# Softmax attention on one core: scores in two accumulated layers of 48 rows, two heads in the two halves of the rows

## The chip, the cores and the metric

One core of one Trainium2 chip runs the whole program in one launch. The metric is the device time of that execution in microseconds (us); lower is better. The engines are named as the profile names them: PE is TensorE (PEld its weight loads), DVE is VectorE, ACT is ScalarE, POOL is GpSimd, SP is SyncE, which only issues transfers here.

## The reference, cut to what matters

The program is four blocks on x of shape (16, 512, 256): softmax attention, a mixture of experts, a gated linear attention, and the mixture of experts again. The change is in the first block alone:

```
q, k, v = (proj(Wq), proj(Wk), proj(Wv))      # 16 heads of 16 dimensions
q, k = _apply_rope(q, k, cos, sin)
scores = jnp.einsum('bhqd,bhkd->bhqk', q, k) / jnp.sqrt(jnp.float32(dk))
attn = jax.nn.softmax(scores, axis=-1)
out = jnp.einsum('bhqk,bhkd->bhqd', attn, v)
return out.transpose(0, 2, 1, 3).reshape(B, S, D) @ Wo.T
```

## The kernel before, in words

`attention_project` normalises x, projects it, rotates q and k, and stores each as three bf16 parts (high, middle, low) whose sum is the fp32 value. `attention_mix` does the rest and is where the change lies.

**Operands.** A product of q and k in nearly fp32 precision is the sum of six products of parts. `Q_PARTS` and `K_PARTS` list the six pairs; each takes 16 rows (the head's dimensions) of the tiles `qs` and `ks`, [128 rows, 16 heads, 512 tokens] in bf16. The first three slots are 48 rows and alone give the maxima; all six are 96 rows. `ROW` puts the slots of even heads at rows 0 to 95, and those of odd heads at 64 to 111 (the first three) and 0 to 47 (the others). Two more rows hold the high and low part of the row maximum in `qs` and -1 in `ks`, so that the score comes out with the maximum subtracted; `SHIFT_ROW` says where. Scores are so a single bf16 product over 98 rows (even heads) or 112 rows (odd heads, some of them filled with -1 times 0): `K_ALL`.

**Steps.** The unit is a pair of heads (even, odd) of a sequence; there are 16 times 8 pairs, and a step of the loop works on several pairs at once, each stage with its own lag in steps (`walk_pairs`). Every engine runs its own list of stages in a written order, and semaphores tie them together. In a step PE does, in this order: `max_products(0)`, two scores, `turn_output` (every second step), `mix_values(1)`, `turn_shift` (every fourth step), `max_products(1)`, two scores, `max_products(2)`, two scores, `mix_values(0)`, `max_products(3)`, two scores, and in single steps `turn_att` and `project`.

- `max_products(t)` (L621): two bf16 products of 48 rows by 512 columns, the even head in rows 0 to 47, the odd one in rows 64 to 111, side by side into two PSUM banks. DVE's `maxima(t)` (L718) reduces both with one instruction.
- `scores(i)` (L649): i is 0 to 3 for the even head's four blocks of 128 keys and 4 to 7 for the odd head's. Each fills one PSUM bank of 512 columns; ACT's `exponentials(i)` (L778) takes the exponential of that bank.
- `mix_values` (L664): four fp32 products side by side, each with 32 output rows.
- `turn_output` (L677), `turn_shift` (L633), `turn_att` (L690), `project` (L703): transposes and the projection of the output, fp32.

**PSUM.** All eight banks are in use: two double banks `ps_m` (maxima, transposed output and shift, projection), three banks `ps_s` (scores, transposed attention), one for `mix_values`. `M_ORDER` and `S_ORDER` give the order in which the users of the two rings take their turn. A user of turn n waits until turn n - 2 (`M_RING`) or n - 3 (`S_RING`) has been drained by DVE or ACT. Each score waits so for itself.

**Transfers.** SP loads the parts of the next sequence while the present one runs, into the other of two tile sets (`first_qs`, `first_ks`, and the two halves of `second`), and, together with POOL, moves the maxima (`m_parts`) into their rows. POOL fills the constant rows of the first set with three memsets (L541 to L543) and ACT those of the second set with three copies.

Of the kernel before, what the change touches and what calls it, by code (L numbers as in the profile page):

```python
# [64 lines left out]

# [269 lines left out]
def attention_mix(nc, dram, x_in, x_out, const):  # L335
# [13 lines left out]

    SHIFT_ROW = (96, 48)  # L350
    K_ALL = (98, 112)

# [14 lines left out]
    M_RING, S_RING = 2, 3  # L367
    M_ORDER = [("max0", 0, 1, 0), ("output", L_OTURN, 2, 1), ("shift", L_TURN, 4, 3), ("max1", 0, 1, 0), ("max2", 0, 1, 0), ("max3", 0, 1, 0),
               ("out0", L_OUT[0], PAIRS, PAIRS - 1), ("out1", L_OUT[1], PAIRS, PAIRS - 1)]
    S_ORDER = [(f"score{i}", L_S, 1, 0) for i in range(8)] + [(f"att{q}", L_ATT[q], PAIRS, PAIRS - 1) for q in range(2)]  # L370
    M_AT, S_AT = turns_in_order(M_ORDER, TOTAL + 16), turns_in_order(S_ORDER, TOTAL + 16)
    M_PERIOD, S_PERIOD = 2 * (4 * PAIRS + 2 + PAIRS // 2 + 2), 2 * (8 * PAIRS + 2)

    with ExitStack() as ctx:
        def sb(name, shape, dt=fp32):
            return ctx.enter_context(nc.sbuf_tensor("a2_" + name, shape, dt))
# [7 lines left out]
        woT = sb("woT", [P, 2, D])  # L384
        fill = sb("fill", [P, 2])
        ident, wo_rows = const["ident_sb"], const["wo_rows"]
        qs = [const["first_qs"], const["second"][:, 0:H * S].rearrange("p (h t) -> p h t", h=H)]
        ks = [const["first_ks"], const["second"][:, H * S:].rearrange("p (h t) -> p h t", h=H)]
        vs = sb("vs", [P, QT, D])
# [84 lines left out]
        def _(sp):  # L474
# [7 lines left out]
            def load_m(seq, u, f):  # L482
                wait(sp, m_drained, m_turn("shift", seq.ahead(4 * f + 3 + L_TURN)) + 1)
                for r in range(2):
                    row, at = SHIFT_ROW[0] + r, r * 4
                    sp.dma_start(qs[u][row:row + 1, f * HALF:(f + 1) * HALF:2, :], m_parts[at:at + 4, f, :]).then_inc(m_even_loaded[f], 16)

            def sequence(seq, b, u, last):
# [5 lines left out]
                if not last:  # L494
                    scores_read(before, 0)
                    load_qk(b + 1, 1 - u, 0, range(MAX_SLOTS), first_loaded)
                    if first:
                        sp.wait_ge(rows_set[1], 3)
                    load_qk(b + 1, 1 - u, 0, range(MAX_SLOTS, len(Q_PARTS)), rest_loaded)
# [14 lines left out]

            sp.wait_ge(rows_set[0], 3)
            for f in range(2):
# [17 lines left out]
        def _(pool):  # L534
            def heads_of(u):
                return va[u][:].rearrange("p t (h w) -> p t h w", w=VW)

            for k, value in enumerate((-1.0, 0.0)):
                nc.gpsimd.memset(fill[:, k:k + 1], value).then_inc(fill_set, 1)
            pool.wait_ge(fill_set, 2)  # L540
# [24 lines left out]
            def load_odd(n, step):  # L565
                if n.k % 4 != 3:
                    return
                f = n.p // 4
                pool.wait_ge(m_drained, m_turn("shift", step) + 1)
                if f == 0 and isinstance(n.base, int):  # L570
                    pool.wait_ge(rows_set[n.u], 3)
                passed_by(pool, pool_passed)
                for r in range(2):
                    row, at = SHIFT_ROW[1] + r, HALF + r * 4
                    pool.dma_start(qs[n.u][row:row + 1, f * HALF + 1:(f + 1) * HALF:2, :], m_parts[at:at + 4, f, :]).then_inc(m_odd_loaded[f], 16)

# [29 lines left out]
        def _(pe):  # L606
# [5 lines left out]
            def max_products(t):  # L612
                def stage(n, step):
                    u = n.u
                    if n.p % 4 == 0 and t == 0:
                        wait(pe, first_loaded[u][n.p // 4], 16 * 4 * MAX_SLOTS * (n.base + u))
                    name = f"max{t}"
                    wait(pe, m_drained, m_turn(name, step) + 1 - M_RING)
                    for e in range(2):
                        rows = slice(ROW[e][0], ROW[e][0] + MAX_SLOTS * DK)  # L620
                        last = nc.tensor.matmul(m_bank(name, step)[:, e, :], qs[u][rows, 2 * n.p + e, t * P:(t + 1) * P], ks[u][rows, 2 * n.p + e, :],  # L621
                                                start=True, stop=True)
                    last.then_inc(m_filled, 1)
                return stage
# [10 lines left out]

            def scores(i):
                def stage(n, step):
                    u, e, t = n.u, i // QT, i % QT
                    if n.p % 4 == 0 and i == 0:
                        f = n.p // 4  # L640
                        pe.wait_ge(rest_loaded[u][f], 16 * 4 * (len(Q_PARTS) - MAX_SLOTS) * (n.base + n.k // PERIOD + 1))
                        pe.wait_ge(rows_set[u], 3)
# [51 lines left out]
            def project(q):  # L694
                def stage(n, step):
# [5 lines left out]
                    for t in range(2):  # L701
                        for c in range(2):
# [3 lines left out]

            walk_pairs(pe, [(0, max_products(0)), (L_S, scores(0)), (L_S, scores(1)), (L_OTURN, turn_output), (L_MIX + 1, mix_values(1)),
                            (L_TURN, turn_shift), (0, max_products(1)), (L_S, scores(2)), (L_S, scores(3)), (0, max_products(2)), (L_S, scores(4)), (L_S, scores(5)), (L_MIX, mix_values(0)),
                            (0, max_products(3)), (L_S, scores(6)), (L_S, scores(7)),
                            (L_ATT[0], turn_att(0)), (L_ATT[1], turn_att(1)), (L_OUT[0], project(0)), (L_OUT[1], project(1))])  # L710

        @block.vector
        def _(dve):
# [29 lines left out]
            def residual(q):  # L743
                def stage(n, step):
# [3 lines left out]
                    if q == 0:  # L748
# [5 lines left out]

            walk_pairs(dve, [(0, maxima(0)), (L_OTURN, normalise), (L_TURN, copy_shift), (0, maxima(1)), (0, maxima(2)), (0, maxima(3)),
                             (L_OUT[0], residual(0)), (L_OUT[1], residual(1))], unrolled=2)

        @block.scalar
        def _(act):
            act.wait_ge(w_turned, 1)  # L760
            nc.scalar.activation(woT[:], ps_s[0][:].rearrange("p (c a) -> p c a", c=2), ACT.Copy).then_inc(w_copied, 1)

            act.wait_ge(fill_set, 2)
            for k in range(2):
                act.wait_ge(const["parts_stored"][k], 16 * SEQS // 2)
            for to, at, k in ((ks[1], slice(32, 64), 0), (qs[1], slice(32, 64), 1), (ks[1], slice(96, 98), 0)):
                heads = to[at, 1 if at.start == 32 else 0::2, :]
                source = fill[at, k:k + 1].rearrange("p (h t) -> p h t", h=1).to_broadcast([at.stop - at.start, H // 2, S])
                nc.scalar.activation(heads, source, ACT.Copy).then_inc(rows_set[1], 1)
# [27 lines left out]
            walk_pairs(act, [(L_S, exponentials(0)), (L_S, exponentials(1)), (L_OCOPY, copy_output)]  # L797
                       + [(L_S, exponentials(i)) for i in range(2, 8)] + [(L_ATT[0], copy_att(0)), (L_ATT[1], copy_att(1))])

# [1249 lines left out]
def program(nc, a):  # L2049
# [37 lines left out]
    with nc.cleanup_on_exit(), ExitStack() as ctx:  # L2087
# [6 lines left out]
        ahead_x = landing["ahead_x"] = ctx.enter_context(nc.sbuf_tensor("ahead_x", [P, WD], fp32))  # L2094
        with (nc.sbuf_tensor("first_qs", [P, 16, S], bf16) as first_qs, nc.sbuf_tensor("first_ks", [P, 16, S], bf16) as first_ks,
              nc.sbuf_tensor("second", [P, 2 * 16 * S], bf16) as second):
# [58 lines left out]
```

## Time and profile before

| | |
|---|---|
| time, three runs | 2562.98 us median, 2553.72 to 2566.74 |
| the profiled execution, span from first to last instruction | 2572.4 us (its time outside the span isn't listed) |
| mean granted TensorE clock | 0.958 of full speed |
| busy over the span | PE 93%, DVE 63%, ACT 53%, POOL 45% |
| attention_mix | about 235 to 1098 us of the span |

A profile row of the timeline gives the start, the duration (to the end of the last of a merged group), the engine, the line of the kernel, and the count behind an x; in brackets stands the idle time before it and what ended it. Matmuls of one engine are pipelined: the start of the next, not the listed end, says when PE was free again.

### The profile page before, as it was taken

To read this page: it belongs to the slowest core of one execution; us is meant where nothing else is said; L and a number is where in the kernel's file an instruction comes from. 1 tells how busy PE (TensorE), PEld (TensorE's weight loads), DVE (VectorE), ACT (ScalarE), POOL (GpSimd) and SP (SyncE) were. 2 spreads that over 40 slices of the span, in tenths; PEclk is the share of its full clock that TensorE was granted. 3 is DMA by queue.
4 is the path that set the end of the run, shared out by engine and by line. 5 is a ranking of instruction groups with operands and counts; after the bars stand their busy time and mean duration, and the time that the engine had idled before them with its cause. 6 is when DMAs were issued, how large, how long until landed. Compare 5 with 4: busy or idle time off the path is not lost. (4 is left out here: it accounts for less than half of the span.)

```text
span 2572.4 us, 48366 instructions
## 1 busy us (share of the span) xinstructions
PE 2397.5 (93%) x14822; PEld 1294.4 (50%) x14822; DVE 1621.6 (63%) x3733; ACT 1370.4 (53%) x2772; POOL 1154.1 (45%) x1497
## 2 busy tenths in 40 slices
PE   8997999999999999979998996999999969998997
PEld 5663233333333333356556764566666645555765
DVE  6777888888888888455552323677777746543332
ACT  5665677667766776646532322555555436532322
POOL 6997110111111111133226775777777723324776
PEclk9997899999999999988998998999999988898999
DMA  6654423232323231145766884011111026585886
GB/s 187 217 189 161 122 81 105 78 107 78 103 82 103 82 99 61 38 132 186 239 220 189 241 197 77 18 38 38 35 38 34 20 75 204 183 283 155 223 228 109
DMA packets 286870, 325.20 MB, mean 126 GB/s; under 512 B 30496, under 2 KB 272368, under 8 KB 286704
## 3 DMA queue, kind: packets, MB, share of 16 engines
q1 hardware_dynamic: 252928, 274.22, 34.0%
q0 software_dynamic: 29184, 46.43, 8.9%
q10 hardware_dynamic: 4592, 2.47, 0.4%
q8 instruction: 89, 1.46, 0.2%
q14 instruction: 77, 0.63, 0.1%
HBM read 217.29 MB, written 105.19 MB: 125 GB/s over the span
## 5 line engine op out<-in xcount | busy, mean ns | idle before, releaser
L718 DVE TENSOR_REDUCE a_row_max<-a_ps_m 128x2 f32<-128x1024 f32 x512 | 607.4, 1219 | 84.2 <-PE a_ps_m L621 79.3
L778 ACT ACTIVATE a_probs<-a_ps_s 128x512 f32<-128x512 f32 x1024 | 536.8, 601 | 206.5 <-PE a_ps_s L649 206.1
L664 PE MATMUL a_ps_o<-a_probs,a_va 128*32 128x512 f32 x2048 | 272.9, 606 | 0.8 <-ACT a_o_sb L787 0.8
L1750 POOL TENSOR_TENSOR b_spread<-b_decay,held_own_sb 128x512 f32<-128x512 f32 x256 | 267.9, 1079 | 8.6 <-DVE b_weight L1811 8.6
L1811 DVE TENSOR_TENSOR b_weight<-b_ps_s,b_spread 128x512 f32<-128x512 f32 x256 | 163.6, 681 | 9.0 <-PE b_ps_s L1952 9.0
L649 PE MATMUL a_ps_s<-first_qs,first_ks 98*128 98x512 bf16 (+1 forms) x512 | 160.8, 395 | 3.3 <-DMA first_qs<-a_m_parts 3.3
L649 PE MATMUL a_ps_s<-second 98*128 98x512 bf16 (+1 forms) x512 | 156.4, 385 | 4.8 <-DMA second<-a_m_parts 2.4
L558 POOL CAST a_high<-a_row_max 128x32 bf16<-128x32 f32 x32 | 6.6, 206 | 316.0 <-DVE a_row_max L718 316.0
L599 POOL DMA_DIRECT2D x<-a_xo x32 | 24.2, 755 | 273.7 <-DVE a_xo L752 271.3
L317 PE MATMUL a_ps_qk<-a_w_qk,a_xnT 128*128 128x512 f32 x256 | 122.2, 600 | 0.0
L1560 DVE SCALAR_TENSOR_TENSOR m2e_h<-m2e_act_g,m2e_xg,m2e_ps_h 128x192 f32<-128x192 f32 x64 | 26.5, 414 | 144.3 <-ACT m2e_act_g L1489 110.8
L1560 DVE SCALAR_TENSOR_TENSOR m1e_h<-m1e_act_g,m1e_xg,m1e_ps_h 128x192 f32<-128x192 f32 x64 | 26.5, 414 | 141.7 <-ACT m1e_act_g L1489 123.0
L621 PE MATMUL a_ps_m<-first_ks,first_qs 48*128 48x512 bf16 x512 | 106.4, 413 | 10.0 <-DVE a_row_max L718 9.3
L621 PEld LDWEIGHTS a_ps_m<-first_ks,first_qs 48*128 48x128 bf16 x512 | 24.7, 93 | 158.2 <-issue 90.5
L1214 PE MATMUL m1f_ps_h<-m_kept,held_ws_gate_up_sb 128*128 128x512 f32 x192 | 104.2, 679 | 0.0
L1888 ACT ACTIVATE b_o_sb<-b_ps_o,held_b_den_eps 128x512 f32<-128x512 f32 x64 | 44.1, 688 | 111.4 <-PE b_ps_o L1962 111.4
L1214 PE MATMUL m2f_ps_h<-m_kept,held_ws_gate_up_sb 128*128 128x512 f32 x192 | 101.7, 665 | 0.0
L621 PE MATMUL a_ps_m<-second 48*128 48x512 bf16 x512 | 99.8, 386 | 0.4
L621 PEld LDWEIGHTS a_ps_m<-second 48*128 48x128 bf16 x512 | 24.5, 92 | 147.6 <-issue 94.8
L1828 DVE TENSOR_TENSOR b_xo<-b_ps_w,b_xt 128x256 f32<-128x256 f32 x63 | 26.8, 425 | 93.4 <-PE b_ps_w L1987 93.4
L200 POOL TENSOR_TENSOR a_qk<-a_rot_cos,a_rot_sin 128x512 f32<-128x512 f32 x64 | 81.4, 1272 | 7.9 <-DVE a_rot_sin L234 7.9
L649 PEld LDWEIGHTS a_ps_s<-second 98*128 98x128 bf16 (+1 forms) x512 | 37.8, 97 | 83.9 <-issue 38.0
(393 smaller groups left out, 5410.4 us busy)
## 6 DMA issues: line engine op xcount, KB each, us to landing
parts<-second SPq DMA_DIRECT2D x16, 1536.0 KB, 6.2
second<-parts SPq DMA_DIRECT2D x384, 64.0 KB
rows<-m_early SPq DMA_DIRECT2D x32, 640.0 KB
m_early<-x SPq DMA_DIRECT2D x31, 512.0 KB
first_qs<-parts SPq DMA_DIRECT2D x192, 64.0 KB, 3.5
first_ks<-parts SPq DMA_DIRECT2D x192, 64.0 KB, 2.9
m_own<-in_L_ffn_w_gate_dram SPq DMA_DIRECT2D x24, 384.0 KB, 6.6
m_own<-in_L_ffn_w_up_dram SPq DMA_DIRECT2D x24, 384.0 KB, 7.2
```

The source lines that it names most:

```text
L200: nc.gpsimd.tensor_tensor(qk[:, u, :], rot_cos[:, u, :], rot_sin[:, u, :], ALU.add).then_inc(qk_done, 1)
L317: last = nc.tensor.matmul(ps_qk[u][:], xnT[:, u, c, :], w_qk[:, c, :], start=c == 0, stop=c == 1)
L621: last = nc.tensor.matmul(m_bank(name, step)[:, e, :], qs[u][rows, 2 * n.p + e, t * P:(t + 1) * P], ks[u][rows, 2 * n.p + e, :], start=Tru ...
L649: nc.tensor.matmul(s_bank(name, step)[:], ks[u][0:K_ALL[e], h, t * P:(t + 1) * P], qs[u][0:K_ALL[e], h, :], start=True, stop=True).then_in ...
L664: last = nc.tensor.matmul(ps_o[VW * j:VW * (j + 1), :], va[n.u][:, t, (h0 + j) * VW:(h0 + j + 1) * VW], probs[:, group % 2, j, t, :], star ...
L718: nc.vector.tensor_reduce(row_max[:, n.k // 4 % 2, t, :, n.p % 4], m_bank(name, step)[:], AX.X, ALU.max).then_inc(m_drained, 1)
L778: nc.scalar.activation(probs[:, group % 2, j, t, :], s_bank(name, step)[:], ACT.Exp, scale=DK ** -0.5).then_inc(s_drained, 1)
L1214: last = nc.tensor.matmul(ps_h[i][:], w_gu[:, c, i, :], x_turned[:, kept_at(r), c, :], start=c == 0, stop=c == 1)
L1560: nc.vector.scalar_tensor_tensor(h[:, i % 2, j, :], act_g[:, i % 2, j, :], xg[:, i % XB, j, D + e:D + e + 1], ps_h[j][:, 1, :], ALU.mult, ...
L1750: nc.gpsimd.tensor_tensor(spread[:, n % 2, heads].rearrange("p h t c -> p (h t) c"), decay[:, n % 3, heads].rearrange("p h (t o) -> p (h t ...
L1811: nc.vector.tensor_tensor(weight[:, n % 2, heads, :], ps_s[r][:].rearrange("p h (j t) -> p (h j) t", t=P), spread[:, n % 2, heads].rearran ...
L1888: nc.scalar.activation(o_sb[:, n % 2, :], ps_o[:].rearrange("p i a -> p (i a)"), ACT.Identity, bias=den_eps[:]).then_inc(o_copied, 1)
```

## The change

Scores are no longer one product over 98 or 112 rows. The six slots of a head now lie in two layers, three slots each: layer 0 has the slots of the maxima, layer 1 the other three and the two shift rows. Even heads have rows 0 to 47 (to 49 in layer 1), odd heads 64 to 111 (to 113), so that a pair's tile is [group, layer, token]. `scores(t)` does the four products of both heads for one block of keys, layer 0 of both and then layer 1 of both, accumulated in the two heads' banks. The wait for the ring now stands once, ahead of the four, for the turn of the second bank. The order of the score turns becomes even, odd, even, odd. The stages of PE are put in another order (`turn_att`, `project` and `mix_values(0)` come between the third scores and `max_products(3)`), and with it the orders of the rings, of DVE and of ACT. Two memsets and two copies fill the constant rows instead of three and three.

```diff
-ROW = ((0, 16, 32, 48, 64, 80), (64, 80, 96, 0, 16, 32))
+LAYERS = 2
+EDGE = 64
...
-                row = ROW[e][slot]
-                yield tile[row:row + 16, f * 8 + e:(f + 1) * 8:2, :], src[e]
+                row = EDGE * e + slot % MAX_SLOTS * 16
+                yield tile[row:row + 16, f * 4:(f + 1) * 4, slot // MAX_SLOTS, :], src[e]
...
-    SHIFT_ROW = (96, 48)
-    K_ALL = (98, 112)
+    PART_ROWS = MAX_SLOTS * DK
+    FILL_ROW = 32
...
-    M_ORDER = [("max0", 0, 1, 0), ("output", L_OTURN, 2, 1), ("shift", L_TURN, 4, 3), ("max1", 0, 1, 0), ("max2", 0, 1, 0), ("max3", 0, 1, 0),
-               ("out0", L_OUT[0], PAIRS, PAIRS - 1), ("out1", L_OUT[1], PAIRS, PAIRS - 1)]
-    S_ORDER = [(f"score{i}", L_S, 1, 0) for i in range(8)] + [(f"att{q}", L_ATT[q], PAIRS, PAIRS - 1) for q in range(2)]
+    M_ORDER = [("max0", 0, 1, 0), ("output", L_OTURN, 2, 1), ("shift", L_TURN, 4, 3), ("max1", 0, 1, 0), ("max2", 0, 1, 0),
+               ("out0", L_OUT[0], PAIRS, PAIRS - 1), ("out1", L_OUT[1], PAIRS, PAIRS - 1), ("max3", 0, 1, 0)]
+    S_ORDER = ([(f"score{i}", L_S, 1, 0) for i in range(6)] + [(f"att{q}", L_ATT[q], PAIRS, PAIRS - 1) for q in range(2)]
+               + [(f"score{i}", L_S, 1, 0) for i in range(6, 8)])
...
-            nc.gpsimd.memset(ks[0][32:64, 1::2, :], -1.0).then_inc(rows_set[0], 1)
-            nc.gpsimd.memset(qs[0][32:64, 1::2, :], 0.0).then_inc(rows_set[0], 1)
-            nc.gpsimd.memset(ks[0][96:98, 0::2, :], -1.0).then_inc(rows_set[0], 1)
-            pool.wait_ge(rows_set[0], 3)
+            for e in range(2):
+                at = slice(EDGE * e + FILL_ROW, EDGE * (e + 1))
+                nc.gpsimd.memset(ks[0][at, :, 1, :], -1.0).then_inc(rows_set[0], 1)
+            pool.wait_ge(rows_set[0], 2)
...
-                    name = f"score{i}"
-                    wait(pe, s_drained, s_turn(name, step) + 1 - S_RING)
-                    h = 2 * n.p + e
-                    nc.tensor.matmul(s_bank(name, step)[:], ks[u][0:K_ALL[e], h, t * P:(t + 1) * P], qs[u][0:K_ALL[e], h, :],
-                                     start=True, stop=True).then_inc(s_filled, 1)
+                    names = [f"score{2 * t + e}" for e in range(2)]
+                    wait(pe, s_drained, s_turn(names[1], step) + 1 - S_RING)
+                    for layer, shift_rows in ((0, 0), (1, 2)):
+                        for e in range(2):
+                            rows = slice(EDGE * e, EDGE * e + PART_ROWS + shift_rows)
+                            last = nc.tensor.matmul(s_bank(names[e], step)[:], ks[u][rows, n.p, layer, t * P:(t + 1) * P], qs[u][rows, n.p, layer, :],
+                                                    start=layer == 0, stop=layer == 1)
+                            if layer == 1:
+                                last.then_inc(s_filled, 1)
...
-            walk_pairs(pe, [(0, max_products(0)), (L_S, scores(0)), (L_S, scores(1)), (L_OTURN, turn_output), (L_MIX + 1, mix_values(1)),
-                            (L_TURN, turn_shift), (0, max_products(1)), (L_S, scores(2)), (L_S, scores(3)), (0, max_products(2)), (L_S, scores(4)), (L_S, scores(5)), (L_MIX, mix_values(0)),
-                            (0, max_products(3)), (L_S, scores(6)), (L_S, scores(7)),
-                            (L_ATT[0], turn_att(0)), (L_ATT[1], turn_att(1)), (L_OUT[0], project(0)), (L_OUT[1], project(1))])
+            walk_pairs(pe, [(0, max_products(0)), (L_S, scores(0)), (L_OTURN, turn_output), (L_MIX + 1, mix_values(1)), (L_TURN, turn_shift),
+                            (0, max_products(1)), (L_S, scores(1)), (0, max_products(2)), (L_S, scores(2)),
+                            (L_ATT[0], turn_att(0)), (L_ATT[1], turn_att(1)), (L_OUT[0], project(0)), (L_OUT[1], project(1)), (L_MIX, mix_values(0)),
+                            (0, max_products(3)), (L_S, scores(3))])
...
-                    group, j, t = n.k // 2, 2 * (n.k % 2) + i // QT, i % QT
+                    group, j, t = n.k // 2, 2 * (n.k % 2) + i % 2, i // 2
```

DVE's list moves the two `residual` stages ahead of `maxima(3)`, ACT's the two `copy_att` stages ahead of the last two exponentials. The transfers of parts and maxima keep their number and size and go to the new places.

## Rows read from the trace of the kernel before

**Rows 1.** The page: span, and section 1, busy time of each engine.
```profile
span 2572.4 us, 48366 instructions
...
PE 2397.5 (93%) x14822; PEld 1294.4 (50%) x14822; DVE 1621.6 (63%) x3733; ACT 1370.4 (53%) x2772; POOL 1154.1 (45%) x1497
```
**Rows 2.** Windows 320 to 1040 us: all work, then L621 alone; clock, DMA share, GB/s last.
```profile
320.00:1040.00 720.00, 714.18 (x4218) 230.33 (x4214) 593.42 (x612) 504.31 (x970) 88.97 (x224) 1.00 0.30 88
...
320.00:1040.00 720.00, 172.85 (x888) 42.51 (x888) 1.00 0.30 88
```
**Rows 3.** Groups by line, 320 to 1040 us: busy us, mean ns, then idle before.
```profile
L778 ACT ACTIVATE a_probs<-a_ps_s 128x512 f32<-128x512 f32 x886 | 464.6, 601 | 170.8 <-PE a_ps_s L649 170.8
```
**Rows 4.** Timeline of PE, 604 to 612.1 us.
```profile
604.40 0.61 PE L649 MATMUL a_ps_s<-first_qs,first_ks 112*128 112x512 bf16 x2
604.85 1.89 PE L703 MATMUL a_ps_m<-a_woT,a_attT 128*128 128x256 f32 x8
606.67 0.39 PE L621 MATMUL a_ps_m<-second 48*128 48x512 bf16 x2
606.99 0.60 PE L649 MATMUL a_ps_s<-first_qs,first_ks 98*128 98x512 bf16 x2
607.73 0.66 PE L677 MATMUL a_ps_m<-held_ident_sb,a_o_sb 128*128 128x128 f32 x4
608.32 1.06 PE L664 MATMUL a_ps_o<-a_probs,a_va 128*32 128x512 f32 x8
609.31 0.39 PE L621 MATMUL a_ps_m<-second 48*128 48x512 bf16 x2
609.64 0.60 PE L649 MATMUL a_ps_s<-first_qs,first_ks 98*128 98x512 bf16 x2
610.17 0.39 PE L621 MATMUL a_ps_m<-second 48*128 48x512 bf16 x2
610.50 0.61 PE L649 MATMUL a_ps_s<-first_qs,first_ks 112*128 112x512 bf16 x2
611.03 1.06 PE L664 MATMUL a_ps_o<-a_probs,a_va 128*32 128x512 f32 x8
612.03 0.39 PE L621 MATMUL a_ps_m<-second 48*128 48x512 bf16 x2
```
**Rows 5.** Timeline, the first scores of the stretch without maxima.
```profile
1053.45 0.82 PE L649 MATMUL a_ps_s<-second 112*128 112x512 bf16 x3
...
1053.87 2.06 ACT L778 ACTIVATE a_probs<-a_ps_s 128x512 f32<-128x512 f32 x4 [0.65 <-PE a_ps_s L649]
1054.52 0.39 PE L649 MATMUL a_ps_s<-second 98*128 98x512 bf16 x1 [0.26 <-ACT a_probs L778]
1054.84 1.07 PE L664 MATMUL a_ps_o<-a_probs,a_va 128*32 128x512 f32 x8
```
**Rows 6.** Timeline, the second score after 609.64 us, and its weight load.
```profile
609.86 0.38 PE L649 MATMUL a_ps_s<-first_qs,first_ks 98*128 98x512 bf16 x1
...
609.65 0.10 PEld L649 LDWEIGHTS a_ps_s<-first_qs,first_ks 98*128 98x128 bf16 x1
```
**Rows 7.** Timeline of PE in the linear attention: scores, then the mixing.
```profile
1724.70 1.15 PE L1952 MATMUL b_ps_s<-b_q_bd,b_kT 32*128 32x256 f32 x16
```
**Rows 8.** Timeline of the start of the stage.
```profile
241.97 3.51 POOL L543 MEMSET first_ks<- 2x4096 bf16 x1
...
254.84 0.21 POOL L558 CAST a_high<-a_row_max 128x32 bf16<-128x32 f32 x1 [5.38 <-DVE a_row_max L718]
...
261.90 1.01 PE L649 MATMUL a_ps_s<-first_qs,first_ks 98*128 98x512 bf16 x2 [1.42 <-DMA first_qs<-a_m_parts]
262.52 1.09 ACT L778 ACTIVATE a_probs<-a_ps_s 128x512 f32<-128x512 f32 x2 [12.84 <-PE a_ps_s L649]
```
**Rows 9.** Windows: PE, PEld, DVE, ACT, POOL busy (x), clock, at start and end.
```profile
265.00:275.00 10.00, 10.00 (x28) 1.53 (x27) 8.31 (x7) 7.05 (x14) 0.00 (x0) 0.50 0.60 171
...
1060.00:1070.00 10.00, 7.64 (x45) 2.42 (x45) 0.68 (x2) 6.82 (x14) 0.00 (x0) 1.00 0.30 101
```

More of the change, by code:

```diff
@@ L384, in attention_mix @@
         woT = sb("woT", [P, 2, D])
-        fill = sb("fill", [P, 2])
+        fill = sb("fill", [P, 1])
         ident, wo_rows = const["ident_sb"], const["wo_rows"]
-        qs = [const["first_qs"], const["second"][:, 0:H * S].rearrange("p (h t) -> p h t", h=H)]
-        ks = [const["first_ks"], const["second"][:, H * S:].rearrange("p (h t) -> p h t", h=H)]
+        qs = [const["first_qs"], const["second"][:, 0:H * S].rearrange("p (g l t) -> p g l t", g=PAIRS, l=LAYERS)]
+        ks = [const["first_ks"], const["second"][:, H * S:].rearrange("p (g l t) -> p g l t", g=PAIRS, l=LAYERS)]
         vs = sb("vs", [P, QT, D])
@@ L484, in load_m @@
                 for r in range(2):
-                    row, at = SHIFT_ROW[0] + r, r * 4
-                    sp.dma_start(qs[u][row:row + 1, f * HALF:(f + 1) * HALF:2, :], m_parts[at:at + 4, f, :]).then_inc(m_even_loaded[f], 16)
+                    row, at = PART_ROWS + r, r * 4
+                    sp.dma_start(qs[u][row:row + 1, f * 4:(f + 1) * 4, 1, :], m_parts[at:at + 4, f, :]).then_inc(m_even_loaded[f], 16)
             def sequence(seq, b, u, last):
@@ L497, in sequence @@
                     if first:
-                        sp.wait_ge(rows_set[1], 3)
+                        sp.wait_ge(rows_set[1], 2)
                     load_qk(b + 1, 1 - u, 0, range(MAX_SLOTS, len(Q_PARTS)), rest_loaded)
@@ L513, in x_rows @@
                 return t[bass.ds(b * S, S), :].rearrange("(t p) d -> p t d", p=P)
-            sp.wait_ge(rows_set[0], 3)
+            sp.wait_ge(rows_set[0], 2)
             for f in range(2):
@@ L536, in heads_of @@
                 return va[u][:].rearrange("p t (h w) -> p t h w", w=VW)
-            for k, value in enumerate((-1.0, 0.0)):
-                nc.gpsimd.memset(fill[:, k:k + 1], value).then_inc(fill_set, 1)
-            pool.wait_ge(fill_set, 2)
-            nc.gpsimd.memset(ks[0][32:64, 1::2, :], -1.0).then_inc(rows_set[0], 1)
-            nc.gpsimd.memset(qs[0][32:64, 1::2, :], 0.0).then_inc(rows_set[0], 1)
-            nc.gpsimd.memset(ks[0][96:98, 0::2, :], -1.0).then_inc(rows_set[0], 1)
-            pool.wait_ge(rows_set[0], 3)
+            nc.gpsimd.memset(fill[:], -1.0).then_inc(fill_set, 1)
+            pool.wait_ge(fill_set, 1)
+            for e in range(2):
+                at = slice(EDGE * e + FILL_ROW, EDGE * (e + 1))
+                nc.gpsimd.memset(ks[0][at, :, 1, :], -1.0).then_inc(rows_set[0], 1)
+            pool.wait_ge(rows_set[0], 2)
             for u in range(2):
@@ L569, in load_odd @@
                 pool.wait_ge(m_drained, m_turn("shift", step) + 1)
-                if f == 0 and isinstance(n.base, int):
-                    pool.wait_ge(rows_set[n.u], 3)
                 passed_by(pool, pool_passed)
                 for r in range(2):
-                    row, at = SHIFT_ROW[1] + r, HALF + r * 4
-                    pool.dma_start(qs[n.u][row:row + 1, f * HALF + 1:(f + 1) * HALF:2, :], m_parts[at:at + 4, f, :]).then_inc(m_odd_loaded[f], 16)
+                    row, at = EDGE + PART_ROWS + r, HALF + r * 4
+                    pool.dma_start(qs[n.u][row:row + 1, f * 4:(f + 1) * 4, 1, :], m_parts[at:at + 4, f, :]).then_inc(m_odd_loaded[f], 16)
             def spread(n, step):
@@ L619, in stage @@
                     for e in range(2):
-                        rows = slice(ROW[e][0], ROW[e][0] + MAX_SLOTS * DK)
-                        last = nc.tensor.matmul(m_bank(name, step)[:, e, :], qs[u][rows, 2 * n.p + e, t * P:(t + 1) * P], ks[u][rows, 2 * n.p + e, :],
+                        rows = slice(EDGE * e, EDGE * e + PART_ROWS)
+                        last = nc.tensor.matmul(m_bank(name, step)[:, e, :], qs[u][rows, n.p, 0, t * P:(t + 1) * P], ks[u][rows, n.p, 0, :],
                                                 start=True, stop=True)
@@ L634, in turn_shift, with scores @@
                 last.then_inc(m_filled, 1)
-            def scores(i):
+            def scores(t):
                 def stage(n, step):
-                    u, e, t = n.u, i // QT, i % QT
-                    if n.p % 4 == 0 and i == 0:
+                    u = n.u
+                    if n.p % 4 == 0 and t == 0:
                         f = n.p // 4
                         pe.wait_ge(rest_loaded[u][f], 16 * 4 * (len(Q_PARTS) - MAX_SLOTS) * (n.base + n.k // PERIOD + 1))
-                        pe.wait_ge(rows_set[u], 3)
+                        pe.wait_ge(rows_set[u], 2)
                         pe.wait_ge(w_copied, 1)
@@ L753, in residual @@
                 return stage
-            walk_pairs(dve, [(0, maxima(0)), (L_OTURN, normalise), (L_TURN, copy_shift), (0, maxima(1)), (0, maxima(2)), (0, maxima(3)),
-                             (L_OUT[0], residual(0)), (L_OUT[1], residual(1))], unrolled=2)
+            walk_pairs(dve, [(0, maxima(0)), (L_OTURN, normalise), (L_TURN, copy_shift), (0, maxima(1)), (0, maxima(2)),
+                             (L_OUT[0], residual(0)), (L_OUT[1], residual(1)), (0, maxima(3))], unrolled=2)
         @block.scalar
@@ L761, in _ @@
             nc.scalar.activation(woT[:], ps_s[0][:].rearrange("p (c a) -> p c a", c=2), ACT.Copy).then_inc(w_copied, 1)
-            act.wait_ge(fill_set, 2)
+            act.wait_ge(fill_set, 1)
             for k in range(2):
                 act.wait_ge(const["parts_stored"][k], 16 * SEQS // 2)
[L766 to L769, printed above, removed]
+            for e in range(2):
+                at = slice(EDGE * e + FILL_ROW, EDGE * (e + 1))
+                source = fill[at, :].rearrange("p (g t) -> p g t", g=1).to_broadcast([EDGE - FILL_ROW, PAIRS, S])
+                nc.scalar.activation(ks[1][at, :, 1, :], source, ACT.Copy).then_inc(rows_set[1], 1)
             def exponentials(i):
                 def stage(n, step):
-                    group, j, t = n.k // 2, 2 * (n.k % 2) + i // QT, i % QT
+                    group, j, t = n.k // 2, 2 * (n.k % 2) + i % 2, i // 2
                     if j == 0:
@@ L797, in _ @@
             walk_pairs(act, [(L_S, exponentials(0)), (L_S, exponentials(1)), (L_OCOPY, copy_output)]
-                       + [(L_S, exponentials(i)) for i in range(2, 8)] + [(L_ATT[0], copy_att(0)), (L_ATT[1], copy_att(1))])
+                       + [(L_S, exponentials(i)) for i in range(2, 6)] + [(L_ATT[0], copy_att(0)), (L_ATT[1], copy_att(1))]
+                       + [(L_S, exponentials(i)) for i in range(6, 8)])
 def moe_front(nc, tag, dram, x_in, x_out, const):
@@ L2094, in program @@
         ahead_x = landing["ahead_x"] = ctx.enter_context(nc.sbuf_tensor("ahead_x", [P, WD], fp32))
-        with (nc.sbuf_tensor("first_qs", [P, 16, S], bf16) as first_qs, nc.sbuf_tensor("first_ks", [P, 16, S], bf16) as first_ks,
+        with (nc.sbuf_tensor("first_qs", [P, 8, LAYERS, S], bf16) as first_qs, nc.sbuf_tensor("first_ks", [P, 8, LAYERS, S], bf16) as first_ks,
               nc.sbuf_tensor("second", [P, 2 * 16 * S], bf16) as second):
```

## The prediction

> **What bounds the kernel now.** I read the page first, then the windows by stage, then PE's timeline. PE is busy in 93% of the span [rows 1]. In the middle of attention_mix it is busy for 714.18 of 720 us, at the full clock of 2.4 GHz (granted 1.00), DVE for 593.42, ACT for 504.31 [rows 2]. The stretch has 888 products for the maxima, eight to a step, so 111 steps of 6.49 us; a step costs DVE 5.35 us and ACT 4.54 us. PE is the bound, DVE has 1.1 us a step in hand, ACT 1.9 us.
>
> PE's timeline says what the step is made of [rows 4]. Between the two mixings of a step lies a close half: maxima at 609.31, scores at 609.64, next maxima at 610.17, so 0.86 us (0.87 on the average I take, since a few of these stall for hundredths). The other half has a mixing in it: 610.17 to 612.03, 1.86 us. Twice both is 5.46 us; the rest of the step, 1.03 us, is the transposes and the projection, spread over eight steps.
>
> The reader is to see the gaps that no column streams through. Two maxima products side by side and a change of shape take 609.31 to 609.64, 0.32 us. Two scores in a row are 0.22 us apart, 609.64 to 609.86 [rows 4, 6], and that is what 512 columns take at this clock. So 0.10 us of the 0.32, and 0.09 to 0.10 of the 0.53 from the first score to the next maxima, go to the change between 48-row and full-height products. Before a projection, of the scores' own shape, the two scores take only 604.40 to 604.85, 0.45 us: no change there. A step has ten such changes: at both ends of two mixings and of what else lies between scores and maxima.
>
> **What the change removes.** Scores now have the shape of the maxima, so the changes between the two go. A close half streams 0.21 us of maxima and twice 0.215 of layers: 0.64 us for 0.87, if nothing waits. A mixing half has 0.21 (maxima), 0.43 (layers), 0.10 (change), 1.00 (mixing with its change out, 608.32 to 609.31): 1.74 us for 1.86, a gain of 0.115 us by unrounded starts. That the second layer costs no more than 0.215 rests on the pair of the maxima itself and on the linear attention, where four rounds of four products in four row strips take 1.15 us from the first start to the last end [rows 7], 0.07 us a product of 256 fp32 columns: strips work beside each other there round after round, each with new weights.
>
> **What it adds.** (1) *The ring.* There are three banks of scores, and the four products now wait at once for both of their banks. The second of them is the bank of the first head of the group before. So PE may not begin a group until the exponential of that first head has ended. Until now PE could fill one further bank meanwhile, and only a single score waited.
>
> The price of that chain stands in the stretch without maxima [rows 5]: three scores start from 1053.45 on, ACT starts on the first at 1053.87, and the fourth, which needs the first one's bank, starts at 1054.52, released by ACT. That is 1.07 us from product to reuse: 0.42 to ACT's start, 0.60 for the exponential [rows 3], 0.05 to PE. In the new group the product that completes the bank, layer 1, starts 0.215 us after layer 0. Start of a group to the earliest start of the next: 0.215 + 1.07 = 1.29 us.
>
> In a mixing half 1.74 us pass anyway, and the wait is hidden. In a close half 0.64 us pass, and 0.65 us of waiting are in the open: 1.29 us for 0.87, a loss of 0.42. Bounds: 0.64 (nothing waits) and 1.78 (as if both exponentials, the second 0.49 us later, were needed). I take 1.29, from a row of this very wait. (ACT starts its exponentials (2.06 - 0.60) / 3 = 0.49 us apart [rows 5].)
>
> Behind the waiting scores PE has the mixing or the next maxima, both ready and both held up. DVE then gets its maxima later, but it has 5.35 us of work for a step that grows. ACT finishes its second exponential 0.64 + 0.49 + 0.60 = 1.73 us after the group's start, before the next group's first result at 1.29 + 0.64 = 1.93. Neither becomes the bound.
>
> (2) *Changes of shape at other places.* In four of eight steps a projection or transpose of attention followed scores directly without a change; it now follows 48-row work, and moves from a close half, where it would have covered the wait, to the mixing half. Before, such a pair of halves was 0.45 + 1.82 (604.85 to 606.67) + 0.32, and 1.86: 4.45 us; now 1.29, and 0.53 + 1.82 + 1.00 + 0.21 = 3.56: 4.85 us, 0.40 more, where a plain pair grows by 0.30: 0.106 us a case by unrounded starts. In four of eight steps `turn_output` follows scores; at 607.73 it starts 0.74 us after those of 606.99, held by the ring of the maxima, while 0.45 would do without a wait and 0.53 with the new change of shape: between a gain of 0.2 and a loss of 0.09, I take a gain of 0.04. The shift's transposes stay behind a mixing: nothing.
>
> (3) *Start.* One memset of 3.51 us less on POOL, one copy less on ACT. The first scores wait for the maxima's transfer [rows 8], which follows DVE's reductions (POOL's cast at 254.84), not the memsets that end at 245.5. Value nothing; at most 3.5 us of gain, if the rest of the loads should be the last to land. In the ramp the clock is at 0.50, that is 1.2 GHz [rows 9]: the chain there is 0.43 (layer 0) + 0.62 (261.90 to 262.52) [rows 8] + 0.65 = 1.70 us for a period of about 1.45 to 1.5 (28 products in 10 us, four a period), some eight times: +2 us.
>
> (4) *Transfers.* Number and size of the loads stay, only their rows move. Nothing, with a bound of 1 us either way: the DMA share is 0.30 [rows 2], and the next sequence's loads have eight steps.
>
> **The sum.** Steps that have both maxima and scores at full clock are about 121.
> - close halves: 242 x 0.415 = +100.5
> - mixing halves: 242 x -0.115 = -27.8
> - projections and transposed attention: 64 x 0.106 = +6.8; `turn_output`: 64 x -0.036 = -2.3
> - ramp +2; the five steps at the end without maxima: close half 1.29 + 0.53 for 1.39 (1053.45 to 1054.84), ten times, less where a transpose lay in it: +3
>
> Together +82 us. The profiled span of 2572.4 us becomes 2654; the median of the runs is 9.4 us under that span, so the time that I predict is 2645 us. The step becomes 7.15 us.
>
> **A rule against it.** A load of weights begins at 609.65 and takes 0.10 us, while the score that began at 609.64 streams through the same rows until 609.86 [rows 4, 6]: here it is hidden. The Trainium skill (TensorE: Matmul & The Clock Gate, Part 3, The mechanism) says that a weight load overlaps a matmul in flight only when its row group differs. By the rule, layer 1 would wait for its load of 0.10 us after layer 0, and so would each boundary of maxima and scores. The rows contradict it for full-height products; for 48-row layers nothing is shown but the strips of [rows 7].
>
> **Rivals.**
> - *The ring doesn't bind, PE only loses its changes.* Close halves at 0.64: 242 x -0.23 = -56, -28 for the mixing halves, +4.5, so -80: 2483 us. For it speaks that PE is the bound and the gaps are real; DVE's 5.35 us would still fit a step of 5.84. Against it stands the fourth score of [rows 5]. The mechanism is the bank's reuse in the close half; it decides at about 0.97 us from group to group in the close half (0.87 and a tenth that the rest gains). Under that the change is faster, over it slower; the chain would have to be a quarter shorter than measured.
> - *Half of it:* a close half near 0.97, for instance if ACT starts earlier than 0.42 after the last layer: about 2563 us.
> - *The halves don't run side by side beyond a single pair,* or loads come into the open. Serial layers make a group 0.85: the close half 1.50, the mixing half 2.17, 242 x 0.64 = +155 on the forecast, 2800 us. A load of 0.10 us in the open, once in the chain of a close half and twice in a mixing half, is 242 x 0.29 = +70: 2715 us.
> - *The clock falls.* PE would stand still for about 0.47 us twice a step. It was granted 1.00 with PE busy for 7.64 of 10 us [rows 9], so I expect it to stay. With a quarter of the stage at 1.2 GHz, about +100: 2745 us.
>
> **Chances.** Forecast 0.80; ring not binding 0.09; half 0.04; serial layers or open loads 0.04; clock 0.03. The forecast's own range, from 0.1 us more or less in a close half and the starts' 3 us: 2617 to 2672. The whole range, 2605 to 2685, leaves out the far rivals. This kernel's measurement tells about 0.5% from no change: faster 0.10, same 0.04, slower 0.86.
>
> **What would show it.** In the profile after: DVE and ACT busy as long as before; the maxima followed by layers 0.21 us later; mixing halves of 1.74 us; in close halves PE idle before the scores, ended by ACT's exponentials, with group starts 1.29 us apart; a step of 7.15 us. Right in the saving and wrong in the ring if close halves are 0.64 us and the waits on ACT are absent; wrong about the layers if group to mixing is 0.96 us, not 0.53.

## Result and profile after

The changed kernel takes 2641.76 us (median of four runs, 2639.81 to 2645.25); the kernel of before, run beside it, 2564.12 us (2553.72 to 2566.74). The ratio is 1.0318, with a 95% interval of 1.0293 to 1.0342: 3.2% slower. Forecast were 2645 us, with 2605 to 2685 as the range. Two executions among the experiments below were far slower than their like (3025.63 us of the kernel of before, 7850.59 us of the run `split_mix`); the ratios leave them out.

The page of the changed kernel, answering to [rows 1]: the span, and section 1.

```profile
span 2640.6 us, 50047 instructions
...
PE 2366.4 (90%) x15846; PEld 1269.5 (48%) x15846; DVE 1622.0 (61%) x3733; ACT 1392.4 (53%) x2771; POOL 1150.6 (44%) x1495
```

PE has 1024 matmuls more and is busy for 31 us less, DVE is busy for as long as before, and the span is 68 us longer. So PE waits more. The windows, answering to [rows 2]: 320 to 1040 us, all work (PE, PEld, DVE, ACT, POOL busy, clock), then the maxima's products alone.

```profile
320.00:1040.00 720.00, 629.19 (x4631) 191.51 (x4628) 539.18 (x553) 480.67 (x884) 77.94 (x197) 1.00 0.28 84
...
320.00:1040.00 720.00, 155.52 (x808) 39.24 (x806) 1.00 0.28 84
```

808 products are 101 steps in 720 us, 7.13 us each for 6.49 (7.155 and 6.482 by the starts of whole cycles of eight steps). PE, busy for 714 of 720 us before, is now idle for 91. The clock is still 1.00. The timeline of PE and ACT shows where PE idles. It answers to [rows 4].

```profile
603.25 0.39 PE L620 MATMUL a_ps_m<-first_ks,first_qs 48*128 48x512 bf16 x2
...
603.47 0.60 PE L650 MATMUL a_ps_s<-first_qs,first_ks 48*128 48x512 bf16 x4
...
603.91 0.38 PE L620 MATMUL a_ps_m<-first_ks,first_qs 48*128 48x512 bf16 x2
604.10 1.08 ACT L781 ACTIVATE a_probs<-a_ps_s 128x512 f32<-128x512 f32 x2
604.75 0.11 PEld L650 LDWEIGHTS a_ps_s<-first_qs,first_ks 48*128 48x128 bf16 x4 [0.96 <-ACT a_probs L781]
604.75 0.61 PE L650 MATMUL a_ps_s<-first_qs,first_ks 48*128 48x512 bf16 x4 [0.47 <-ACT a_probs L781]
605.29 0.16 PEld L667 LDWEIGHTS a_ps_o<-a_probs,a_va 128*32 128x32 f32 x8 [0.43 <-issue]
605.29 1.06 PE L667 MATMUL a_ps_o<-a_probs,a_va 128*32 128x512 f32 x8
...
606.29 0.39 PE L620 MATMUL a_ps_m<-first_ks,first_qs 48*128 48x512 bf16 x2
...
606.52 0.60 PE L650 MATMUL a_ps_s<-first_qs,first_ks 48*128 48x512 bf16 x4
```

Read it from the group of scores at 603.47. The maxima before it started only 0.22 us earlier: no change of shape between them, and none to the maxima at 603.91, 0.44 us later, for four products. Then PE has nothing until 604.75, although the next scores were ready to be issued; what ends the wait is the exponential that started at 604.10. The two group starts are 1.28 us apart. The mixing half, 604.75 to 606.52, is 1.77 us and has no wait. The instructions of line L650 say how often:

```profile
its engine sat idle before it (us, times) until:
  ACT a_probs L781: 358.3, 511
```

(The sum adds the idle time of PE and that of its weight loads.) At the end of the stage the last projection, L706 here and L703 before, tells the stage's growth; of before, of after:

```profile
L703 PE MATMUL a_ps_m<-a_woT,a_attT x256: 377/379/483, 345.3 to 1100.8; 128*128 128x256 f32 x128
```
```profile
L706 PE MATMUL a_ps_m<-a_woT,a_attT x256: 379/379/483, 351.7 to 1185.5; 128*128 128x256 f32 x128
```

The stage is 84.7 us longer, the span only 68.2: in the one profiled execution of before, everything behind attention took 1471.6 us, in that of after 1455.1. In the profiled executions of all seven experiments it was between 1454 and 1461, so it is the one of before that stands out; why, the traces don't show. The medians, 77.6 us apart, lie in between.

### The profile page after: what moved, and what is told of

Its sections match the earlier page's. It is cut to its first block and busy times, and to the rows that moved or that the text cites. A ratio compares the mean times of both kernels' runs of the same rounds, so it can differ in the third digit from the quotient of the medians.

```text
span 2640.6 us, 50047 instructions
## 1 busy us (share of the span) xinstructions
PE 2366.4 (90%) x15846; PEld 1269.5 (48%) x15846; DVE 1622.0 (61%) x3733; ACT 1392.4 (53%) x2771; POOL 1150.6 (44%) x1495
## 3 DMA queue, kind: packets, MB, share of 16 engines
q8 instruction: 91, 1.49, 0.2%
## 5 line engine op out<-in xcount | busy, mean ns | idle before, releaser
L781 ACT ACTIVATE a_probs<-a_ps_s 128x512 f32<-128x512 f32 x1024 | 555.7, 595 | 283.0 <-PE a_ps_s L650 280.4
L650 PE MATMUL a_ps_s<-first_qs,first_ks 48*128 48x512 bf16 (+1 forms) x1024 | 158.9, 390 | 57.4 <-ACT a_probs L781 55.5
L650 PE MATMUL a_ps_s<-second 48*128 48x512 bf16 (+1 forms) x1024 | 154.2, 380 | 59.7 <-ACT a_probs L781 58.2
L650 PEld LDWEIGHTS a_ps_s<-second 48*128 48x128 bf16 (+1 forms) x1024 | 39.0, 94 | 141.8 <-ACT a_probs L781 123.3
L650 PEld LDWEIGHTS a_ps_s<-first_qs,first_ks 48*128 48x128 bf16 (+1 forms) x1024 | 39.6, 95 | 138.7 <-ACT a_probs L781 121.3
```

The lines of the kernel that those rows point to most:

```text
L650: last = nc.tensor.matmul(s_bank(names[e], step)[:], ks[u][rows, n.p, layer, t * P:(t + 1) * P], qs[u][rows, n.p, layer, :], start=layer = ...
L781: nc.scalar.activation(probs[:, group % 2, j, t, :], s_bank(name, step)[:], ACT.Exp, scale=DK ** -0.5).then_inc(s_drained, 1)
```

## Experiments

Two theories stood against each other. *Ring:* the wait for both banks at once lets no group start before the exponential of the group before, and that costs the time. *Work:* the wait is harmless, and what costs is the doubled number of products, the new shape or the new order. All times below are medians over several rounds, each beside the kernel of before (2562 us in the first four, 2564 us in the last three). Step lengths and gaps are worked out from the starts in each trace, between 320 and 1000 us.

**1. Two banks set free, not used (`bank3`)**

```diff
-        ps_m = [pb(f"ps_m{u}", [P, 2, S]) for u in range(M_RING)]
+        ps_m = [pb(f"ps_m{u}", [P, 1, S]) for u in range(M_RING)]
...
-                    for e in range(2):
+                    for e in range(1):
...
-                nc.vector.tensor_reduce(row_max[:, n.k // 4 % 2, t, :, n.p % 4], m_bank(name, step)[:], AX.X, ALU.max)
+                nc.vector.tensor_reduce(row_max[:, n.k // 4 % 2, t, :, n.p % 4], m_bank(name, step)[:].to_broadcast([P, 2, S]), AX.X, ALU.max)
```

(the loop over e is that of `max_products`)

> The changed kernel, with the maxima's product made for the even head alone, into a single bank, which VectorE reads twice (the odd head's maxima are so left out). VectorE's and ScalarE's work and every wait stay as they are; two PSUM banks come free and aren't used. It is the ground for the next run. Both theories (the wait for both score banks costs the time; the layers or the new order cost it) expect the time of the changed kernel, 2642 us within 8, since the odd head's product ran beside the even one's.

Measured: 2650.09 us, ratio 1.0337 (1.0303 to 1.0372), just outside the 8 us that I had allowed. The step is 7.15 us as in the changed kernel, and so are the two halves together (1.28 + 1.76 us), so within the steps the odd head's product was free.

**2. A fourth bank for the scores (`bank4`)**

```diff
-    M_RING, S_RING = 2, 3
+    M_RING, S_RING = 2, 4
```

> The same with a ring of four score banks instead of three, so that a group of four products waits for nothing younger than the group before the last. Theory of the ring: the close half goes from 1.28 us to the 0.66 us that its own work takes, 242 times, so 150 us less than the run before: 2490 us, up to 20 more if VectorE (5.35 us of a step of 5.9) now makes PE wait at times. Rival, that layers, shape or order are what costs: the time of the run before, 2642 us, within 10.

Measured: 2537.69 us, ratio 0.9904 (0.9878 to 0.9930). One number changed, and 112 us went, more than the change had cost. That settles the ring against the work theory. It is also less than 150: the step fell to 6.33 us, where PE's own work would need 5.86. From maxima to maxima a plain close half takes 0.66 us, as expected, and a plain mixing half 1.74: together 2.40 us, in which PE waits for nothing. The missing 0.47 us a step, 57 us in all, lie for the most part in the other halves. With the output's transpose a mixing half takes 2.70 us where 2.33 would do, with the shift's transposes 2.74 for 2.27, with the projection 4.01 for 3.68 (means; what would do is the plain half and what each adds in the changed kernel). What PE itself waited for in that stretch says why (engine, tile and line, for whom, us in total, times, longest):

```profile
PE a_ps_m L632 <- DVE a_row_max L721: 10.8, 27, 0.4
PE a_ps_m L680 <- DVE a_row_max L721: 9.2, 39, 0.2
PE a_ps_m L706 <- DVE a_row_max L721: 7.3, 27, 0.3
```

L632, L680 and L706 are the third users of the maxima's ring, which still has two turns. In the timeline the output's transpose needs the bank of the maxima two turns earlier:

```profile
611.73 0.39 PE L620 MATMUL a_ps_m<-second 48*128 48x512 bf16 x1
...
612.39 0.38 PE L620 MATMUL a_ps_m<-second 48*128 48x512 bf16 x1
...
613.43 0.66 PE L680 MATMUL a_ps_m<-held_ident_sb,a_o_sb 128*128 128x128 f32 x4 [0.23 <-DVE a_row_max L721]
```

That is 1.70 us from product to reuse: 0.42 to VectorE's start, 1.22 for the reduction, the rest to PE. So the next limit is a ring too, that of the maxima.

**3. The wait alone, in the old kernel (`both_wait`)**

```diff
                     name = f"score{i}"
-                    wait(pe, s_drained, s_turn(name, step) + 1 - S_RING)
+                    if i % 2 == 0:
+                        wait(pe, s_drained, s_turn(f"score{i + 1}", step) + 1 - S_RING)
```

> The kernel of before, where each two scores in a row now wait at once for both of their banks; shapes, layers and order as before. Theory of the ring: no group may start before the exponential of the first score of the group before has ended, 0.42 + 0.60 + 0.05 = 1.07 us after its start, so the close half goes from 0.87 to 1.07 us, 242 times 0.20 = 48 us more than before: 2612 us. Rival, that the wait is harmless and the cost lies in the layers: no change, 2564 us.

Measured: 2596.70 us, ratio 1.0127 (1.0101 to 1.0153): 35 us by the medians, without a layer or a new shape. In PE's timeline the scores at 604.29 and 605.37 are the pair:

```profile
604.29 0.61 PE L650 MATMUL a_ps_s<-first_qs,first_ks 98*128 98x512 bf16 x2
604.83 0.39 PE L621 MATMUL a_ps_m<-second 48*128 48x512 bf16 x2
605.37 0.61 PE L650 MATMUL a_ps_s<-first_qs,first_ks 112*128 112x512 bf16 x2 [0.15 <-ACT a_probs L779]
```

1.08 us, as expected. The 48 us were too many for two reasons. I had counted all 242 close halves; in this order 50 of the 201 of the stretch have a projection or a transpose in them. With the projection they stay at 2.59 us, the wait hidden, but with the transpose they go from 1.30 to 1.57, so that all close halves still cost about 46 us. And since PE comes later to the ring of the maxima, it waits less there: mixing halves with the output's transpose fall from 2.48 to 2.41 us and those with the shift's from 2.50 to 2.39, about 8 us in all. The step grew by 0.31 us, 38 us over 121 steps.

**4. The old order with the new shape (`old_order`)**

```diff
-                            (0, max_products(1)), (L_S, scores(1)), (0, max_products(2)), (L_S, scores(2)),
-                            (L_ATT[0], turn_att(0)), (L_ATT[1], turn_att(1)), (L_OUT[0], project(0)), (L_OUT[1], project(1)), (L_MIX, mix_values(0)),
-                            (0, max_products(3)), (L_S, scores(3))])
+                            (0, max_products(1)), (L_S, scores(1)), (0, max_products(2)), (L_S, scores(2)), (L_MIX, mix_values(0)),
+                            (0, max_products(3)), (L_S, scores(3)),
+                            (L_ATT[0], turn_att(0)), (L_ATT[1], turn_att(1)), (L_OUT[0], project(0)), (L_OUT[1], project(1))])
```

(and the rings' orders, DVE's and ACT's as they were before)

> The changed kernel with the order of stages and turns of the kernel before: attention's transposes and the projection again behind the last scores of a step, that is in the close half. Theory of the ring: what lies in the close half is hidden by its wait. The projection (twice in eight steps, 32 cases) costs 4.30 us for the two halves instead of 4.95: 32 times -0.6 = -20 us. The transposes take a turn in the ring of scores, so that the next scores wait for the odd head's exponential too, 1.78 us for 1.28: nearly no gain, -3 us. In all 2619 us. Rival, that the order brought the changed kernel something or is the loss: over 2650 or near 2564 us.

Measured: 2628.81 us, ratio 1.0267 (1.0230 to 1.0303), 13 us under the changed kernel by the medians. The halves add up to that. With a projection: 2.68 + 1.76 = 4.44 us for 1.28 + 3.70 = 4.98, 32 times -0.54 = -17. With the transpose: 1.77 + 1.76 for 1.28 + 2.35, 32 times -0.10 = -3. The output's transpose again meets the ring of the maxima, 2.44 for 2.35 us, 64 times +0.09 = +6. Together -14. The 2619 us that I expected left out the output's transpose, and I had taken the projection's close half 0.12 too short. The transpose's case is visible in PE's and ACT's timeline:

```profile
587.76 0.60 PE L649 MATMUL a_ps_s<-second 48*128 48x512 bf16 x4
...
588.29 0.66 PE L692 MATMUL a_ps_s<-held_ident_sb,a_att 128*128 128x128 f32 x4
588.39 1.09 ACT L780 ACTIVATE a_probs<-a_ps_s 128x512 f32<-128x512 f32 x2 [0.67 <-PE a_ps_s L649]
588.88 0.39 PE L619 MATMUL a_ps_m<-first_ks,first_qs 48*128 48x512 bf16 x2
589.36 0.60 ACT L796 ACTIVATE a_attT<-a_ps_s 128x512 f32<-128x512 f32 x1
589.53 0.61 PE L649 MATMUL a_ps_s<-second 48*128 48x512 bf16 x4 [0.26 <-ACT a_probs L780]
```

The transpose takes a bank, so the scores at 589.53 wait for both exponentials, which end at 588.39 + 1.09 = 589.48: 1.77 us from group to group for a forecast of 1.78. This is the upper bound that the prediction set for a close half.

**5. A shorter exponential (`short_exp`)**

```diff
-                    nc.scalar.activation(probs[:, group % 2, j, t, :], s_bank(name, step)[:], ACT.Exp, scale=DK ** -0.5)
+                    nc.scalar.activation(probs[:, group % 2, j, t, 0:256], s_bank(name, step)[:, 0:256], ACT.Exp, scale=DK ** -0.5)
```

> The changed kernel, with each exponential taken over the first 256 of its 512 columns (the mixing reads these twice, so that its work stays; the rest of the probabilities is left out). Theory of the ring: the chain from a group's start to the next is shorter by what the exponential is, about 0.37 us for 0.60 (the copies of 256 columns in the trace take 0.37). The close half goes from 1.28 to about 1.05 us, 190 plain ones in the steady stretch and some 240 in all: -55 us, 2587 us. Rival, that ScalarE isn't in the chain and PE's own work or VectorE sets the close half: 2642 us, within 8.

Measured: 2597.49 us, ratio 1.0125 (1.0084 to 1.0167), 44 us under the changed kernel where 55 were expected. The exponential shrank by 0.21 us (0.60 to 0.38 us on average), not 0.23, and the close half by as much, 1.28 to 1.07; over 242 of them that is 52 us, of which the halves with a projection or the shift's transposes and what lies behind the stage give some back. ScalarE is busy for only 309 of 680 us here, so it isn't its throughput that matters, but its delay: in the timeline (PE, ACT) the groups at 604.86 and 605.93 are 1.07 us apart.

```profile
604.86 0.60 PE L650 MATMUL a_ps_s<-first_qs,first_ks 48*128 48x512 bf16 x4
...
605.48 0.39 PE L620 MATMUL a_ps_m<-second 48*128 48x512 bf16 x2
605.49 0.66 ACT L781 ACTIVATE a_probs<-a_ps_s 128x256 f32<-128x256 f32 x2 [1.67 <-PE a_ps_s L650]
605.93 0.61 PE L650 MATMUL a_ps_s<-first_qs,first_ks 48*128 48x512 bf16 x4
```

**6. Old shape with four banks (`old_bank4`)**: the edits of 1 and 2 in the kernel of before.

> The kernel of before (scores over 98 and 112 rows, its own order) with the same two alterations as the run with four score banks: the odd head's maxima left out, VectorE reading the even head's bank twice, and a ring of four for the scores. It gives the ground for what the shape alone brings. Theory (changes of shape cost 0.10 us each and PE is the bound): its close half stays at 0.86 and its mixing half at 1.86 us, the time near 2558 us, so that the four-bank run of the new shape, 2538 us, is 20 us better. Rival, that the shape brings nothing and four banks brought all of it: 2538 us here too.

Measured: 2556.02 us, ratio 0.9977 (0.9959 to 0.9995), step 6.47 us. The fourth bank is worth little to the old kernel, which waits singly. Against 2537.69 us for the new shape with four banks the shape and order bring 18 us, where PE's work alone would have given some 75 (5.86 us a step for 6.47): the rest is the 57 us that experiment 2 found at the ring of the maxima.

**7. Each mixing in two halves (`split_mix`)**

```diff
+                    cols = slice(half * S // 2, (half + 1) * S // 2)
...
-                        last = nc.tensor.matmul(ps_o[VW * j:VW * (j + 1), :], va[n.u][:, t, (h0 + j) * VW:(h0 + j + 1) * VW],
-                                                probs[:, group % 2, j, t, :], start=t == 0, stop=t == QT - 1)
+                        last = nc.tensor.matmul(ps_o[VW * j:VW * (j + 1), cols], va[n.u][:, t, (h0 + j) * VW:(h0 + j + 1) * VW],
+                                                probs[:, group % 2, j, t, cols], start=t == 0 and half == 0, stop=t == QT - 1 and half == 1)
```

(in PE's order a half of a mixing stands behind each of the four groups; in ACT's, `copy_output` stands behind exponentials 0 to 3)

> The changed kernel with each mixing cut into two halves of 256 columns, one in every gap between two groups of scores, the whole computation done. The four gaps of a step are then alike: 0.43 layers + 0.10 + 0.45 half a mixing + 0.10 + 0.21 maxima = 1.30 us, against the ring's 1.28, so no wait is in the open, at the price of four more changes of shape. Theory of the ring: the step goes from 7.15 to about 6.3 us; VectorE, with 1.22 us for each of the maxima, has 0.08 us a gap in hand and may take some of it back: 2545 us, between 2530 and 2575, so a little faster than before (2562 us). Rival, that cutting costs as much as the wait (more loads, more changes, VectorE as the new bound): 2600 us or more.

Measured: 2588.16 us, ratio 1.0083 (1.0055 to 1.0112): 54 us better than the changed kernel, still slower than before, and my range missed. The plain gaps are as meant, with no wait for an exponential in the open:

```profile
603.06 0.39 PE L620 MATMUL a_ps_m<-second 48*128 48x512 bf16 x2
603.29 0.60 PE L650 MATMUL a_ps_s<-first_qs,first_ks 48*128 48x512 bf16 x4
603.82 0.64 PE L668 MATMUL a_ps_o<-a_probs,a_va 128*32 128x256 f32 x8
604.39 0.39 PE L620 MATMUL a_ps_m<-second 48*128 48x512 bf16 x2
604.61 0.60 PE L650 MATMUL a_ps_s<-first_qs,first_ks 48*128 48x512 bf16 x4
```

1.32 us from group to group. But the step is 6.70 us, not 6.3. Four plain gaps are 5.29. The transposes and the projection add 1.11 (over eight steps 4 x 0.59 for the output's transpose, 2 x 1.93, 2 x 0.59 and 2 x 0.75 for projection, attention's and the shift's transposes). Three things are new. What PE waited for between 320 and 1000 us names two of them (us in total, times, longest):

```profile
PE a_ps_m L620 <- issue: 14.5, 6, 2.5
PE a_ps_o L668 <- ACT a_o_sb L792: 9.6, 24, 0.5
```

The first is a stall that no other run has: PE stands idle for 2.2 to 2.6 us once in 16 steps, where its loop begins anew (between 320 and 1040 us its longest idle time in the other runs is 1.2 us). That is 0.15 us a step.

```profile
649.98 0.64 PE L668 MATMUL a_ps_o<-a_probs,a_va 128*32 128x256 f32 x8
653.03 0.39 PE L620 MATMUL a_ps_m<-first_ks,first_qs 48*128 48x512 bf16 x2 [2.40 <-issue]
```

The second comes of this run's own order: the first half of a mixing waits for ACT's copy of the output (L792), which now stands behind four exponentials. Four times in 16 steps such a gap is 0.4 to 0.6 us longer: 0.12 a step. The third is the clock. After every second stall it was granted at 0.50, that is 1.2 GHz, for 3.4 us, about 1.5 us after PE had started again; 0.04 a step.

```profile
439.40:442.80 3.40, 3.40 (x20) 0.86 (x22) 2.08 (x3) 1.63 (x4) 1.07 (x2) 0.52 0.00 1
```

(PE, PEld, DVE, ACT, POOL busy, clock, DMA share, GB/s.) Together 6.71 us.

## Why the prediction was right

- *PE was the bound, and the changes of shape its slack:* right. From maxima to scores there are now 0.22 us for 0.32, and from a group to the next maxima 0.44 for 0.54. The mixing half fell by 0.097 us (1.859 to 1.762); forecast were 0.115.
- *The second layer costs no more than the second score did:* right. Four products take 0.44 us from group to maxima. The weights of layer 1 come in under layer 0: layer 0 runs from 603.47 us to the start of layer 1 at 603.69, and the loads of 50 rows, those of layer 1, are these:

```profile
603.47 0.10 PEld L650 LDWEIGHTS a_ps_s<-first_qs,first_ks 50*128 50x128 bf16 x2
```

  The Trainium skill (TensorE: Matmul & The Clock Gate, Part 3, The mechanism) says that a weight load overlaps a matmul in flight only when its row group differs. The trace doesn't agree, and the 2715 us forecast for loads in the open didn't come.
- *The ring makes a close half 1.29 us:* right, 1.283, and shown by taking it away (112 us), by adding it alone to the old kernel (35 us) and by shortening ScalarE's part of it by 0.21 us a close half (44 us). The chain read in [rows 5] gave it to a hundredth.
- *Neither DVE nor ACT becomes the bound:* right for this kernel. ACT's busy time rose by 22 us with as many exponentials: each takes 0.543 us of it (439.1 us for 809 in the window) for 0.524 before [rows 3], probably since fewer of them now start while another runs.
- *The other places:* a projection's pair of halves took 4.98 us, not 4.85. I had carried over the 1.82 us from a projection's start to what follows; behind 48-row scores it is 1.92. The change of shape after it is not the reason: in `old_order` the maxima follow the projection, as before, and it is 1.93 us. Why it takes 0.10 us longer isn't shown. The output's transpose lost its wait: 2.35 us for 2.48.
- *The sum:* +82 us for the stage; it was +84.7. In part that is luck. By the means of the trace the close halves brought +99 us for +100.5, the mixing halves -25 for -27.8, projections and transposed attention +12 for +6.8, and the shift's transposes, which I had put at nothing, -3: the errors nearly cancel. The median's +77.6 us is smaller than the stage's growth, and the difference lies outside the stage.
- *The rival "ring doesn't bind"* would not have given 2483 us even with the ring away: with a fourth bank it was 2538. I had argued that 5.35 us of VectorE's work fit a step of 5.84. They do fit, but the two turns of the maxima's ring make PE wait wherever a third user needs a bank whose reduction still runs. With three banks nothing of this shows.
- *Clock:* right. It stayed at 1.00 with PE idle for 13% of the stretch.

## What to carry to other kernels

A shared wait for several buffers is as late as the youngest of them: before joining single waits into one, count the ring's slots against what the group takes at once, and time one product to the reuse of its bank. Here three banks with groups of two left no bank for PE to work ahead in, and the gain in PE's own work went into a stall twice as large. Put the long work between the groups that the ring ties. And that an engine's work fits the whole step doesn't say that nobody waits for it: check each user of its buffers against the time from product to reuse.

## What the runs showed of the hardware beyond that

- Changing between products of 48 rows and of full height costs PE 0.10 us at either end (0.32 for 0.22 us from maxima to scores, 0.54 for 0.44 from scores to maxima). Two strips of the rows work side by side at full rate over two accumulated layers (four products of 512 columns in 0.44 us at 2.4 GHz).
- Cutting the mixing gave a step 16 products more, and each return to the start of PE's loop of 16 steps left PE idle for 2.2 to 2.6 us. In the same run one queue of instructions moved 155 packets of together 2.54 MB; in the changed kernel it was 91 and 1.49 MB, and in the other runs 88 to 91:

```profile
q8 instruction: 155, 2.54, 0.4%
```
```profile
q8 instruction: 91, 1.49, 0.2%
```

By the starts of these packets in the traces, the changed kernel has none between 438 and 1147 us, while PE goes round its loop. With the cut mixing they go on through the whole stage, about one in 11 us, and at each of the six stalls one starts 2.6 to 2.9 us before PE's next product. So the longer loop is loaded anew on each pass, and the shorter one isn't. That PE's stall is the wait for such a packet fits the times, but wasn't tried by itself.
